# A transformer block on one core: the fill ahead of the step loop written out in an order of its own

## What is computed

```python
x = L0_attn_x                                   # 8 batches, 256 positions, 128 features
mod = (silu(c) @ wmod).reshape(8, 6, 1, 128)    # sa, ca, ga, sb, cb, gb
ga = (2 * (ga >= 0) - 1) * maximum(abs(ga), 0.25)     # gb likewise
h = layernorm(x) * (1 + ca) + sa
x = x + ga * attention(h)                       # 16 heads of 8, causal, a bias linear in position
h = layernorm(x) * (1 + cb) + sb
x = x + gb * ffn(h)   # router softmax over 8 experts; expert 0 has the weights w1, b1, w2, b2,
                      # the other seven the same weights, changed where |w| is among
                      # the 5% largest or 5% smallest
```

## Time and profile before

| what | value |
|---|---|
| median of 3 runs | 246.72 us (245.69 to 247.44) |
| the profiled execution | 246.49 us, span 244.8 us |
| TensorE busy | 217.0 us (89%) |
| VectorE busy | 195.2 us (80%) |
| ScalarE busy | 169.4 us (69%) |
| GpSimd busy | 143.2 us (58%) |

### The profile page before, as it was taken

One profiled execution on the slowest core, in us unless ns is written; L12 is line 12 of the kernel. 1 busy time (PEld: TensorE's weight loads), 2 busy tenths in 40 slices (PEclk: granted clock), 3 DMA queues, 4 the chain that ended last, 5 costly groups with the idle time before them and its releaser, 6 DMA issues.

```text
span 244.8 us, 5563 instructions
## 1 busy us (share of the span) xinstructions
PE 217.0 (89%) x1848; PEld 143.6 (59%) x1864; DVE 195.2 (80%) x621; ACT 169.4 (69%) x401; POOL 143.2 (58%) x232
## 2 busy tenths in 40 slices
PE   5898888989988989987979879997998999999993
PEld 2454555655655766564656646664554687764783
DVE  2549999999899999999999888884897394764474
ACT  2336767999999988998968967974668552354220
POOL 7652051495887986997585433563859808190710
PEclk9999999999999979999999999999999999999999
DMA  6544673894843722714431500000000001010011
GB/s 198 102 137 143 162 195 98 210 252 130 201 119 98 173 76 83 187 49 122 119 88 60 139 3 5 0 3 3 3 0 1 3 0 44 3 43 0 3 43 44
DMA packets 19155, 20.45 MB, mean 84 GB/s; under 512 B 1367, under 2 KB 17382, under 8 KB 18062
## 3 DMA queue, kind: packets, MB, share of 16 engines
q1 hardware_dynamic: 18438, 19.76, 30.8%
q10 hardware_dynamic: 688, 0.33, 0.5%
HBM read 14.70 MB, written 5.26 MB: 82 GB/s over the span
## 4 chain that ended last, share of the span: by engine, by line
PE 49%; DVE 30%; ACT 11%; issue 8%; DMA 1%; DVEq 0%; ACTq 0%
PE bank L891 12%; PE bank L873 8%; DVE nmax L1165 8%; PE bank L688 4%; DVE msk L1136 4%; ACT msk L560 4%; PE bank L790 3%; DVE nmax L1161 3%; ACT PT L548 3%; DVE cand L1148 2%; PE bank L965 2%; PE bank L856 2%; PE bank L769 2%; PE bank L836 2%; PE bank L747 2%
## 5 line engine op out<-in xcount | busy, mean ns | idle before, releaser
L489 POOL TENSOR_SCALAR_AFFINE_SELECT PT<-PT 128x256 f32<-128x256 f32 (+1 forms) x96 | 45.3, 486 | 38.1 <-ACT PT L548 36.1
L548 ACT ACTIVATE PT<-bank 128x512 f32<-128x512 f32 x96 | 54.8, 608 | 4.2 <-PE bank L764 2.7
L1165 DVE TENSOR_REDUCE nmax<-bank 128x2 f32<-128x512 f32 x64 | 43.3, 681 | 1.9 <-PE bank L747 1.5
L560 ACT ACTIVATE msk<-w2a,cand 128x512 bf16<-128x512 f32 x60 | 43.0, 729 | 0.0
L462 POOL TENSOR_TENSOR ex<-eul,lg 128x32 f32<-128x32 f32 x4 | 21.7, 5436 | 20.2 <-DVE lg L1227 20.2
L560 ACT ACTIVATE msk<-w1a,cand 128x512 bf16<-128x512 f32 x31 | 22.9, 737 | 6.2 <-DVE cand L1148 5.9
L769 PE MATMUL bank<-Qs,Ks 80*128 80x256 bf16 x128 | 24.8, 276 | 0.7 <-ACT PT L548 0.4
L747 PE MATMUL bank<-Ks,Qs 78*128 78x256 bf16 x128 | 24.5, 274 | 0.0
L1136 DVE TENSOR_SCALAR_CACHE_REDUCE msk<-w1a,cand 128x512 bf16<-128x512 f32 x31 | 23.1, 746 | 1.1
L743 PE MATMUL bank<-mask 128*128 128x256 bf16 x64 | 17.8, 279 | 5.5 <-DVE nmax L1165 4.7
L1161 DVE TENSOR_REDUCE nmax<-bank 128x4 f32<-128x512 f32 x32 | 21.6, 675 | 1.1 <-PE bank L740 0.8
(11 more groups left out here) (200 smaller groups left out, 511.4 us busy)
## 6 DMA issues: line engine op xcount, KB each, us to landing
Qs<-parts SPq DMA_DIRECT2D x7, 576.0 KB
Ks<-parts SPq DMA_DIRECT2D x7, 576.0 KB
parts<-part SPq DMA_DIRECT2D x7, 384.0 KB, 2.8
rows_bc<-rows_out SPq DMA_DIRECT2D x8, 192.0 KB, 7.9
x_all<-in_x SPq DMA_DIRECT2D x8, 128.0 KB, 7.0
parts<-part SPq DMA_DIRECT2D x8, 128.0 KB, 2.9
out<-ob SPq DMA_DIRECT2D x3, 256.0 KB, 2.3
w_sb<-in_w SPq DMA_DIRECT2D x2, 256.0 KB, 5.1
```

Source lines behind the costliest of these rows:

```text
L489: gp.affine_select(out=v, in_=v, compare_op=ALU.is_ge, fill=0.0, base=0, pattern=[[0, v.shape[1]], [1, P]], channel_multiplier=-1).then_in ...
L548: act.activation(PT[:, e % 2, j], psE[u % 2][:, :], ACT.Exp).then_inc(q["exp_done"], 1)
L560: act.activation(msk[:, col], w[:, :], ACT.Sign, bias=cand[:, col:col + 1].bitcast(F32), scale=-(1.0 - 2.0 ** -24), accum_out=acc[:, col:c ...
L1165: ve.tensor_reduce(nmax[:, b % 2, 1, h:h + 2], bank.rearrange("p (h k) -> p h k", h=2), axis=AX.X, op=ALU.max, negate=True).then_inc(q["ma ...
```

## The change

The loop now starts at t = 0. What its first ten steps did is written out ahead of it, on each engine as a straight list:

- SyncE loads block 0 of x first, then c and the modulation weights, block 1 ahead of w1 and w2, and block 2 ahead of the vectors.
- VectorE takes the statistics of block 0, its negated mean and its normalising before it copies the weights; it copies the vector columns last, after the counts of bit 2, and computes the gate signs before it decides on bit 1.
- TensorE computes the values of batch 0 straight after its projection and before the matmul of the modulation rows, transposes the vectors after the total of bit 0 (into the bank `psO`), and has other numbers of spares between. The values of batch 1, which the loop did at t = −1, are computed in step 0, at its end. The router's sums are done in step 0 and its constants in step 1.
- ScalarE takes |w1| after the parts of batch 0, and scales batch 1 between the two sign counts of bit 0. The copy of batch 1's values stays in step 0, behind the sign counts of bit 2.
- GpSimd does blocks 1 and 2 and then the lower parts of batch 1.

```diff
-T_FIRST = -10
-ROWS_STEP, VEC_STEP, SIZE_STEP, BIAS_STEP, WO_STEP = -3, -4, 7, 31, 7
+ROUTER_STEP, SIZE_STEP, BIAS_STEP, WO_STEP = 0, 7, 31, 7
...
+            block_in(0)
             sp.dma_start(c_in[:, :], c).then_inc(q["c_in"], 16)
-            block_in(0)
             sp.dma_start(wmod_sb[:, :], wmod).then_inc(q["wmod_in"], 16)
+            block_in(1)
             sp.dma_start(w1_sb[:, :], w1).then_inc(q["w1_in"], 16)
...
+            rstd(NBLK, 2 * NBLK, 2)
+            normal(1)
+            rstd(2 * NBLK, 3 * NBLK, 3)
+            normal(2)
+            lower_parts(1)
...
+            scaled(0)
+            first_parts()
+            act.wait_ge(q["w1_in"], 16)
+            act.activation(w1a[:, :], w1_sb[:, :], ACT.Abs).then_inc(q["act_set"], 1)
+            value_copy(0)
+            sign_count(0, 2, w1a)
+            scaled(1)
+            sign_count(0, 3, w2a)
+            high_parts(1)
+            sign_count(1, 2, w1a)
+            sign_count(1, 3, w2a)
+
+            for t in range(T_END):
                 n = sel_bit(t)
...
                 b = batch_at(t - 1, AT_V)
                 if b is not None:
+                    value_copy(b)
...
+            turned(0)
+            spare(3)
+            projected(0)
+            spare(4)
+            values(0)
+            mm(psE[1][0:B, 0:512], c_s[:, :], wmod_sb[:, 2 * D:6 * D], start=True, stop=True).then_inc(q["pe_set"], 1)
+            turned(1)
+            spare(2)
+            projected(1)
+            spare(2)
+            total(0)
+            spare(4)
+            vectors()
+            total(1)
+            spare(2)
+
+            for t in range(T_END):
                 n = sel_bit(t)
                 s_unit(t, 0)
...
+                if t == 0:
+                    values(1)
                 b = batch_at(t, AT_T)
                 if b is not None:
...
+            ln1(0)
+            v.wait_ge(q["ln_stat"], 1)
+            ve.tensor_scalar(nm1[:, 0:NBLK], mv1[:, 0:NBLK, 0], -1.0, None, op0=ALU.mult).then_inc(q["neg_mean"], 1)
             v.wait_ge(q["act_set"], 1)
...
+            first_split()
+            v.wait_ge(q["w2_in"], 16)
+            then_self(absolute(w2a[:, :], w2_sb.rearrange("p c d -> p (c d)")))
+            first_cand()
+            dve_counts(0)
+            gate_sizes()
+            ln1(2)
+            decide(0)
+            next_cand(0)
+            dve_counts(1)
+            after_next(0)
+            remainder(1)
+            other_mod_rows()
+            gate_signs()
+            decide(1)
+            next_cand(1)
+            dve_counts(2)
+            after_next(1)
+            vector_columns()
+
+            for t in range(T_END):
```

More of the change, by code:

```diff
@@ L494, in _ @@
                 b = batch_at(t, AT_N1)
-                if b:
+                if b is not None:
                     normal(b)
                 b = batch_at(t, AT_SPLIT)
-                if b is not None and b >= OWN_SPLIT:
+                if b is not None:
                     lower_parts(b)
@@ L902, in total, with turned, projected, values @@
                 mm(psX[:, 0:4], ones_f[:, :], acc[:, :], start=True, stop=True).then_inc(q["tot_done"], 1)
-            for t in range(T_FIRST, T_END):
+            def turned(b):
+                pe.wait_ge(q["n1_done"], b + 1)
+                if b == 0:
+                    pe.wait_ge(q["dve_set"], SETS["silu"])
+                else:
+                    pe.wait_ge(q["v_out"], b)
+                for i in range(NBLK):
+                    last = tr(psQ[:, i * P:(i + 1) * P], n1[:, b % 2, i, :], ident[:, :])
+                last.then_inc(q["t_done"], 1)
+            def projected(b):
+                pe.wait_ge(q["h1_done"], b + 1)
+                for a in range(2):
+                    bank = psS[1][:, 0:S] if a and b == 0 else psQ[:, a * S:(a + 1) * S]
+                    last = mm(bank, wqkT[:, a, :], h1T[:, b % 2], start=True, stop=True)
+                    if a == 0 and b == 0:
+                        last.then_inc(q["q0_done"], 1)
+                last.then_inc(q["qk_done"], 1)
+            def values(b):
+                pe.wait_ge(q["res_done"], b + 1)
+                for i in range(NBLK):
+                    last = mm(psQ[:, i * P:(i + 1) * P], h1T[:, b % 2, i * P:(i + 1) * P], wvT[:, :], start=True, stop=True)
+                last.then_inc(q["v_done"], 1)
+            turned(0)
[14 more added lines that the diff above has]
+            for t in range(T_END):
                 n = sel_bit(t)
@@ L949, in _ @@
                     last.then_inc(q["y_done"], 1)
+                if t == 0:
+                    values(1)
                 b = batch_at(t, AT_T)
                 if b is not None:
[L952 to L959, removed]
+                    turned(b)
                 b = batch_at(t, AT_QK)
                 if b is not None:
[L962 to L970, removed]
+                    projected(b)
                 b = batch_at(t, AT_V)
                 if b is not None:
[L973 to L979, removed]
+                    values(b)
+                if t == ROUTER_STEP:
                     router_sums()
@@ L1060, in _ @@
             ds(ve.tensor_tensor(c_s[:, :], psQ[:, 0:B], c_e[:, :], op=ALU.mult))
-            ln1(0)
+            v.wait_ge(q["neg_mean"], 1)
+            v.wait_ge(q["ln_rstd"], 1)
+            for i in range(NBLK):
+                last = ve.tensor_scalar(n1[:, 0, i, :], x_all[:, 0, i, :], nm1[:, i:i + 1], rs1[:, i:i + 1],
+                                        op0=ALU.add, op1=ALU.mult)
+            last.then_inc(q["n1_done"], 1)
             v.wait_ge(q["pe_set"], 2)
@@ L1079, in _ @@
             ds(ve.tensor_copy(woT[:, :], psO[:, 0:P]))
+            ln1(1)
             def first_split():
@@ L1312, in perturb_b2, with remainder @@
                 tiers(psX[:, 0:P], psX[:, P:2 * P], b2_bc[:, :], b2p_bc[:, :], b2t[:, :], K_B2, "b2p_done")
-            for t in range(T_FIRST, T_END):
+            def remainder(b):
+                v.wait_ge(q["hi_done"], b + 1)
+                v.wait_ge(q["split_done"], b)
+                pq = psQ.rearrange("p (a t) -> p a t", a=2)
+                ve.tensor_tensor(resid[:, :, :], pq, part8[:, b % 2, 0:4:3, :], op=ALU.subtract).then_inc(q["res_done"], 1)
+            first_split()
[17 more added lines that the diff above has]
+            vector_columns()
+            for t in range(T_END):
                 n = sel_bit(t)
@@ L1335, in _ @@
                 b = batch_at(t, AT_SPLIT)
[L1336 to L1343, removed]
+                if b is not None:
+                    remainder(b)
                 maxima(t, 2)
```

101 lines of the change are left out of this document (38 added, 63 removed).

## The result

| kernel | median | ratio to before, 95% interval |
|---|---|---|
| before | 246.95 us (245.69 to 247.44, 4 runs) | |
| changed | 250.28 us (250.11 to 251.59, 4 runs) | 1.0162 [1.0118, 1.0205] |

The median lies inside the range that was given (246.0 to 250.7), but 1.3 us above the forecast of 249.0, and on the other side of the 1% bound than the likeliest case. A ratio is reckoned from the single executions and leaves slow ones out, so it need not equal the ratio of two medians.

The account below looks back on a forecast made before the run. No single engine bounds the kernel; the main loop's start and new waits on the search's slack-free round trip count. Against 246.49 us: −2.1 + 2.34 + 0.2 + 2.1 = +2.5, so 249.0 us; own range 247.8 to 250.0, given range 246.0 to 250.7.

Parts of the forecast that it names:

- the likeliest case: Whole kernel: a time within 1% of before, given a chance of 0.56.
- parts 1 to 3: Fill up to the search's first round: bit 1's counts start at 17.2 instead of 20.34, 3.1 us earlier.
- part 4: Between bit 1's and bit 2's counts: gate signs ahead of the decision add 1.09 us, leaving 2.1 us of gain.
- parts 5 and 6: Step 0: ScalarE's copy waits for batch 1's values, +2.34 us; half clock on TensorE adds 2.1 us.
- Part 1: Batch 0 up to its parts: transposes at about 7.1, projection 0.5 us earlier, second remainder ending at 11.75 or 11.6.
- part 3: Search's first round: bit 0's total 2.1 us after batch 1's transposes, bit 1's counts at 17.2, 3.1 us earlier.
- part 2: Values of batch 0 and transposes of batch 1: transposes end between 13.6 and 14.9, taken as 14.2.
- part 6: TensorE's clock: after a long pause before bit 2's total, step 0 runs at 1.2 GHz, +2.1 us.
- all of it ahead of the copy: Step 0 on TensorE: half clock's +2.4 us falls wholly before ScalarE's awaited copy of batch 1's values.
- third rival: Steps 0 and 1: clock not regained in step 0, step 1 also at half clock; 2.4 more, 251.4 us; chance 0.08.
- second rival: Search steps: unseen slack absorbs the copy's wait, up to 2.1 us kept, 244.3 us; chance 0.10.
- The first: Rival for step 0: TensorE's clock stays full, 246.9 us (246.3 to 247.6); chance 0.20.

Follow-up runs that it names:

- e10: The changed kernel, unchanged, run again for a second profile: 251.29 us.
- e2: The changed kernel with the three gate-sign instructions back behind bit 2's counts: 248.32 us, 1.0118 against before.
- e9: The changed kernel with five small GpSimd memsets delaying its subtraction of batch 1's lower parts: 249.47 us, 1.0080 against before.
- e1: The changed kernel with batch 1's values computed ahead of the first score tile, before the loop: 246.95 us, 1.0053 against before.
- e3: The changed kernel with 18 spare matmuls between the first score tile and bit 2's total: 247.84 us, 1.0111 against before.
- e8: The changed kernel with batch 1's values before the loop and 16 spares ahead of bit 2's total: 245.09 us, 0.9974 against before.
- e4: The kernel before with only batch 1's values moved to the end of step 0: 250.89 us, 1.018 against before.
- e6: The changed kernel with batch 1's values before the loop and gate signs behind bit 2's counts: 0.9953 against before; median of all twelve executions 247.89 us.
- e5: The kernel before, unchanged, run again for a second profile: that execution took 246.81 us.
- e7: As e6, with eight spares between the first score tile and bit 2's total: 244.12 us, 0.9892 against before.

## Why the prediction fell short

Its terms against the table above:

| term | forecast | measured | what shows it |
|---|---|---|---|
| parts 1 to 3, bit 1's counts earlier | −3.1 | −4.2 (e10: −2.8) | profiles |
| part 4, gate signs ahead of the decision | +1.1 | +2.1 | e2, e9 |
| bit 2 to bit 3 | 0 | +0.1 | profiles |
| parts 5 and 6, step 0 | +4.4 | +4.2 | e1, e3, e8 |
| step 1 | +0.2 | +1.8 | e1, e3, e4 |
| sum, rounded | +2.5 | +4.0 | |

The measured terms come from one profile of each kernel, with e10 as the second of the changed one.

**Parts 1 to 3.** Part 1 was wrong, and part 3 right. With block 0 of x loaded ahead of c, TensorE's first matmul waited for c until 3.73 us (2.81 before), a price that the prediction left out, so the transposes of batch 0 began at 8.03, not 7.1, and the projection at 9.07, not 8.8:

```profile
3.73 0.27 PE L705 MATMUL bank<-ident,c_in 8*128 8x8 f32 x1 [3.73 <-DMA c_in<-in_c]
...
9.07 1.13 PE L942 MATMUL bank<-h1T,wqkT 128*128 128x256 f32 x4
```

What more than made up for it was TensorE's speed: that projection took 1.13 us, not 2.07, the transposes of batch 1 ended at 13.2, before the 13.6 to 14.9 that part 2 gave, and bit 1's counts stood at 16.1 instead of 17.2. In e10 the projection took 1.91 us and the counts stood at 17.6. So 2.8 us of the gain stand in both profiles, and the rest came with the earlier full speed of the one execution, which is luck. From the transposes' end to the total of bit 0 it took 2.2 us, forecast 2.1, so what the search now waits for was read rightly.

**Part 4** had the right place and missed one thing: it priced the three instructions by their row of before, where the last ran alone. Moved, it met GpSimd's subtraction and took 0.84 us more (e9). The rows that could have warned were in the trace of before, where the instruction that writes the next candidate took 0.55 us instead of the 0.16 that it took at 21.68, beside the same GpSimd operation:

```profile
23.20 1.16 POOL L425 TENSOR_TENSOR part<-resid,part 128x512 bf16<-128x512 f32 x1
...
23.84 0.55 DVE L1152 TENSOR_TENSOR nxt<-cand,probe 128x4 uint32<-128x4 uint32 x1
```

That bit 2's counts then stood at 21.00, forecast 21.1, is luck: they started 1.1 us too early and took 1.0 us too long. In e10, without the early start, they stood at 22.29.

**Parts 5 and 6 are right for step 0.** From total to total it is 7.64 us against 7.65 forecast; the +4.2 of the table goes by the starts of the counts. The bare wait in ScalarE's queue is 5.40 (e3, e4; forecast 5.55). The half clock came in step 0 as was said, and filling the long pause with spares kept it away (e3, e8). What was not seen: with the wait removed and the clock still half, TensorE's own work would have taken its place (e1, 5.53). So neither cause alone would have freed the step: of the 4.4 us between 7.64 and 3.20, undoing the wait alone gives 2.1 and undoing the half clock alone 2.2.

**The step that failed is the last one of part 6**, "all of it ahead of the copy": half clock was given to step 0 alone. Step 1 was left at full clock, at +0.2 us for the router, and half clock there was put into the third rival at 0.08. Measured, step 1 took 5.62 us instead of 3.79, +1.8, and nothing of it is the router, since with the same router instructions e1, e6 and e8 take 3.72 or 3.73. In the changed kernel the clock came back at 28 us and was lost again at 31, in e10 at 29 and 32. TensorE is busy for all of the 7 us from 31 to 38 us, so the half clock went straight into the time. The third rival named the outcome but not its course: it had the clock not come back in step 0, and its sign, the clock at bit 3's total (30.97 us), stood at 1.00; its price was 2.4.

What brings the loss of step 1 is the move of batch 1's values. Every profile that lost the clock there has ScalarE's copy wait for them (the changed kernel, e2, e4, e9, e10), and none without that wait lost it (before, e1, e5 to e8). e1 settles it, since it takes the wait away from the changed kernel and leaves step 0 at half clock. It does not need half clock in step 0, since e4 has none. But the wait alone is not enough: e3 has it and keeps its clock. With 1.6 us more for step 1, the forecast would have been 250.6 and slower. Beside it, part 4 was 1.0 us short and the early start 1.1 us too good, and these two cancel.

The second rival, hidden slack, is refuted by e4: one copy made to wait, and the kernel was 1.8% slower. The first, full clock in step 0, is e3's case: it gave 246.9 us, 0.2% above before, and e3 measured 1.1%, the collision of part 4 among it. In the chances, 0.28 for the forecast above 249.2 is 0.45 of its 0.62, not the 0.4 that is named.

## What to carry to other kernels

When a producer is moved, look at the consumer's place in its queue, not only at its semaphore: a copy that had found its values ready now held back the search behind it. After each new wait ask what TensorE does meanwhile; here a pause cost twice, once as itself and once through the clock of the next steps, and spares in it kept the clock. Whether such spares are free is not shown: the stretch behind bit 5 is 0.7 to 2.2 us longer than before's in the profiles of the three kernels with added spares (e3, e7, e8), and no run here separates that from the chance of where the clock dips later. And undo the parts of a change one at a time: this one held a gain of 2.4 to 4.8 us in the fill (bit 1's counts at 15.50 to 17.90 instead of 20.34) that two misplaced items more than took back; with both put right and eight spares it is 1.1% faster than before (e7).

## What the runs showed of the hardware that was not expected

After pauses of 0.57 and 0.86 us the granted clock fell to 0.50 in the changed kernel, and after 0.56 and 0.85 in its repetition, while after pauses of 0.56 and 0.85 us in e3 it stayed at 1.00. The length of a single pause doesn't decide; what else does was not separated here.

A GpSimd subtraction of 1.28 us held back a VectorE operation of 8 partitions by 0.84 us.

In the fill of the kernel before the windows give a granted clock of 1.00 from 3 us on (for 10 to 25 us see the earlier trace rows), while the projection took 2.07 us at 9.28 and 1.03 at 17.76. There the prediction read half clock from the length of rows, not from the column; why the column does not show it stays open.

Beyond step 1 the executions agree within 0.3 us over 211 us, except in some with a later dip of the clock. Before's own profile has a dip and is at most 0.3 us longer there, e9 has one and is no longer than before, e3 and e7 are 0.7 us longer than before and e8 2.2.
